# Building a graph layer's cell counts inside an earlier edge pass instead of next to their use

## The reference

```python
# attention layer
e = leaky_relu(a1[src] + a2[dst]); m = segment_max(e, dst)
ex = exp(e - m[dst]); out = segment_sum(ft[src] * ex / segment_sum(ex, dst)[dst], dst)
# mean layer
agg = segment_sum(x[edge_src], edge_dst)      # out = x @ W_self + (agg / deg) @ W_neigh + b
```

## Time and profile before

| | |
|---|---|
| median of 3 runs | 2354.08 us (2348.93 to 2357.85) |
| span of the profiled execution | 2350.5 us |
| busy | PE 1674.7, DVE 1397.8, POOL 1035.9, ACT 472.2 us |
| `stage_flash`, first gather to the next stage | 74 to 1124 us |
| `stage_experts` | 1124 to 1424 us |
| `blend` | 1424 to 1503 us |
| `stage_dense` | 1503 to 1900 us |
| `stage_experts2` and the output | 1900 to 2350 us |

### The profile page before, as it was taken

How to read it: one execution, slowest core, us unless ns; L and a number is a source line. 1 busy time by engine, 2 the same in 40 slices (tenths; PEclk the granted TensorE clock), 3 DMA queues, 4 the chain that set the end, 5 groups by cost and what they waited for, 6 DMA issues and landing times. The chain is left out here.

```text
span 2350.5 us, 34313 instructions
## 1 busy us (share of the span) xinstructions
PE 1674.7 (71%) x8967; PEld 1121.0 (48%) x8967; DVE 1397.8 (59%) x4277; ACT 472.2 (20%) x1077; POOL 1035.9 (44%) x1088
## 2 busy tenths in 40 slices
PE   4466666666667666666337993799999965599970
PEld 3222222222222222222226882599999964488860
DVE  6466666666666666667555115698888845211118
ACT  2100000000000000000322432533333312122222
POOL 1577777777777777773272332000000016222221
PEclk9677776776776767767558996899999976799985
DMA  7455555555555555553325863499000022566644
GB/s 203 108 145 145 142 145 138 144 142 142 145 144 144 145 145 145 145 144 92 99 97 153 246 211 130 103 246 244 2 0 0 0 48 83 160 214 215 214 140 160
DMA packets 255967, 321.42 MB, mean 137 GB/s; under 512 B 64440, under 2 KB 207522, under 8 KB 255767
## 3 DMA queue, kind: packets, MB, share of 16 engines
q1 hardware_dynamic: 198464, 174.84, 27.0%
q0 software_dynamic: 50208, 138.59, 21.6%
q10 hardware_dynamic: 7238, 7.39, 1.1%
HBM read 217.43 MB, written 103.68 MB: 137 GB/s over the span
## 5 line engine op out<-in xcount | busy, mean ns | idle before, releaser
L520 POOL DMA_INDIRECT f_buf<-ftab,scol x806 | 766.2, 951 | 288.5 <-issue 245.3
L920 PE MATMUL ps<-nb_parts,g_counts 128*120 128x256 bf16 x2550 | 305.9, 273 | 0.0
L603 PE MATMUL ps<-ident,f_left 128*128 128x512 f32 x204 | 189.5, 1084 | 135.5 <-ACT f_left L664 135.5
L920 PEld LDWEIGHTS ps<-nb_parts,g_counts 128*120 128x120 bf16 x2550 | 282.8, 133 | 1.9
L612 PE MATMUL ps<-f_diag,f_ones 128*128 128x512 f32 x204 | 186.7, 1070 | 88.6 <-DVE f_diag L754 88.6
L790 DVE TENSOR_TENSOR f_buf<-f_buf,ps 128x1024 f32<-128x1024 f32 x204 | 235.4, 1217 | 17.7 <-ACT ps L673 17.7
L1015 DVE TENSOR_SCALAR g_cell_hot<-nb_table,g_now 128x250 bf16<-128x250 int16 x816 | 231.9, 284 | 0.1
L1014 DVE TENSOR_SCALAR g_src_hot<-nb_table,g_now 128x128 bf16<-128x128 int16 x816 | 203.6, 249 | 27.8 <-PE ps L911 27.5
L751 DVE TENSOR_REDUCE ps<-ps 128x8 f32<-128x1024 f32 x51 | 62.9, 1233 | 250.0 <-PE ps L606 250.0
L1194 POOL MEMSET y_r_half<- 128x25 f32 x1 | 0.1, 120 | 415.1 <-POOLq L874 415.1
L952 ACT CAST g_counts<-ps 128x500 bf16<-128x500 f32 x204 | 115.0, 580 | 222.4 <-PE ps L911 221.3
(11 more groups left out here) (466 smaller groups left out, 2549.4 us busy)
## 6 DMA issues: line engine op xcount, KB each, us to landing
y_wts<-in_L_ffn_w_dram SPq DMA_DIRECT2D x68, 512.0 KB, 4.0
xs<-zero_rows SPq DMA_DIRECT2D x33, 1032.0 KB, 15.0
x_wts<-in_L_ffn_expert_w_dram SPq DMA_DIRECT2D x84, 256.0 KB, 3.2
xs<-zero_rows SPq DMA_DIRECT2D x51, 403.1 KB, 5.0
f_buf<-ftab,scol POOLq DMA_INDIRECT x806
y_xr<-xs SPq DMA_DIRECT2D x34, 258.0 KB, 3.8
x_xr<-xs SPq DMA_DIRECT2D x28, 258.0 KB, 3.1
f_st<-state SPq DMA_DIRECT2D x51, 132.5 KB, 2.3
```

Of the source, the lines that this page charges most:

```text
L520: nc.gpsimd.indirect_dma_start(out=buf[u][:, j, :], out_offset=None, in_=s.ftab, in_offset=bass.IndirectOffsetOnAxis(ap=s.scol[:, b * CB + ...
L603: nc.tensor.matmul(wide[:, w:w + 4, :], left[b.side][:].rearrange("p j h -> p (j h)"), bc(s.ident[:], 1, 4), start=True, stop=False)
L920: last = nc.tensor.matmul(acc[b.side], counts[b.side][:, t, :], s.parts[:, t, n, :], start=t == 0 and n == 0, stop=t == NT - 1 and n == PA ...
```

## The change

Counts are built in `stage_flash` and stored in DRAM; `stage_dense` loads and multiplies them.

- `stage_flash`, additions per batch. DVE: `cell_hots`, 16 one-hots of 250 columns from the int16 table in four pieces of four, and `bring_cells`. ACT: `bring_rows`, and `row_hots` in two halves, each 8 ACTIVATEs (Abs of iota minus the source row, 128 columns) and one ACTIVATE (Relu of 1 minus that, 1024 columns), which make `src_hot`; `lay` in four pieces. PE: `count` in four pieces of four matmuls. SP: `keep_counts`, one store of 128 x 4000 bytes.
- `stage_flash`, alterations. The diagonal (L754) and the one 16x1024 mask (L738) go. `spread_chunks` becomes 8 float32 transposes and 8 bfloat16 matmuls of 128 columns; `fold_chunks` becomes 2 bfloat16 matmuls of 512 columns and 8 float32 matmuls of 128 columns whose weights are the chunk maxima, broadcast. `mask_chunks` makes two 128x128 comparisons, and `bring` and `spread_tops` lose one instruction each. The two products share two PSUM banks, so the counts can have two.
- `stage_dense`. Ten blocks of 3 or 6 batches: 3, seven of 6, 3, 3. The features' parts are now the weights, 128 columns at a time, and the counts move, up to 480 columns: 150 matmuls a block. DVE adds each pair of chunks, 408 of them, to `accT` on its own (address read, add of 128 x 20, drain). ACT issues the loads of blocks ahead, and the first block is loaded during `blend`.
- `table_parts` is cut to `turn_parts`; its tables move into `stage_open`.

The orders in `stage_flash` after the change (the diff, cut to its core):

```diff
 # TensorE
                 def step(b, nxt, after, later):
                     bring(b)
+                    count(b, 0)
+                    look_up(b)
+                    count(b, 1)
                     if nxt:
                         spread_chunks(nxt)
-                    look_up(b)
-                    if nxt:
                         fold_chunks(nxt)
+                    count(b, 2)
+                    count(b, 3)
                     sum_up(b)
                     place_sums(b)
 # ScalarE
+            def row_hots(b, half):
+                n = CB // 2
+                act.wait_ge(built, b.quarter(2 * half + 1 - UNITS))
+                for j in range(n):
+                    nc.scalar.activation(rows_to[:, j, :], s.iota[:], ACT.Abs, bias=now_row[b.side][:, half * n + j:half * n + j + 1])
+                act.drain()
+                nc.scalar.activation(src_hot[:, half * n:(half + 1) * n, :], rows_to[:], ACT.Relu, scale=-1.0, bias=one[:]).then_inc(row_ready, UNITS // 2)
+                act.drain()
                 def step(b, nxt, after, later):
+                    lay(b, 0)
+                    lay(b, 1)
                     if nxt:
+                        bring_rows(nxt)
+                        row_hots(nxt, 0)
                         copy_left(nxt)
                     weigh(b)
+                    lay(b, 2)
+                    lay(b, 3)
                     if nxt:
+                        row_hots(nxt, 1)
                         fade(nxt)
                     keep_sums(b)
 # VectorE
+            def cell_hots(b, k):
+                dve.wait_ge(built, b.quarter(k - UNITS))
+                for j in range(k * UC, (k + 1) * UC):
+                    last = nc.vector.tensor_scalar(cell_hot[:, j, :], s.table[:], now_cell[b.side][:, j:j + 1], None, ALU.is_equal)
+                last.then_inc(hot_ready, 1)
                 def step(b, nxt, after, later):
+                    cell_hots(b, 0)
                     spread_tops(b)
                     if nxt:
                         mask_batch(nxt)
+                    cell_hots(b, 1)
+                    if nxt:
                         chunk_tops(nxt)
                     arguments(b)
+                    cell_hots(b, 2)
+                    cell_hots(b, 3)
                     messages(b)
                     if nxt:
+                        bring_cells(nxt)
                         batch_tops(nxt)
                     if after:
                         mask_chunks(after)
                     merge(b, nxt)
```

More of the change, by code:

```diff
@@ L87 @@
 NPS = 27 * 128
[L88 to L91, removed]
+GC = 2
+GB = CB // GC
+NGR = NC // GC
 UNITS = GB // 2
@@ L607, in spread_chunks @@
[L607 to L612, removed]
-                pe.wait_ge(masks_ready, b.count())
-                for h in range(0, HEADS, 4):
-                    last = nc.tensor.matmul(wide2[:, h:h + 4, :], s.nident[:], bc(bmask[b.side][:].rearrange("p j w -> p (j w)"), 1, 4), start=False, stop=True)
+                pe.wait_ge(mx_ready, b.count(1))
@@ new lines, in fold_chunks @@
+            def fold_chunks(b):
+                pe.wait_ge(mx_ready, b.count())
+                pe.wait_ge(masks_ready, b.count())
+                for w in range(0, W8, 4):
+                    nc.tensor.matmul(wide2[:, w:w + 4, :].rearrange("p w (j h) -> p w j h", h=HEADS), s.nident[:], bc(bmask[b.side][:, w:w + 4, :], 3, HEADS), start=True, stop=False)
+                for w in range(W8):
+                    last = nc.tensor.matmul(wide2[:, w, :], mx[b.side][:, w:w + 1].broadcast_to([128, 128]), s.ident[:], start=False, stop=w % 4 == 3)
@@ new lines, in _ @@
+            for m in range(len(BLOCKS)):
+                multiply(m)
+            pe.wait_ge(added, len(BLOCKS))
+            with pe.Fori(1, rounds2(pe)) as q:
+                with pe.Fori(0, NBT) as i:
+                    pe.wait_ge(late_hots, late(q, i))
+                    for j in range(CB):
+                        last = nc.tensor.matmul(late_cells[j // UC][:, j % UC // GC, :], src_hot[:, j, :], cell_hot[:, j, :], start=j % GC == 0, stop=j % GC == GC - 1)
+                    last.then_inc(late_built, 1)
+                    pe.wait_ge(late_laid, late(q, i))
+                    for c in range(2):
+                        for t in range(NT):
+                            for n in range(PARTS):
+                                last = nc.tensor.matmul(late_sums[c], s.parts[:, t, n, c * 128:(c + 1) * 128], counts[:, t, :],
+                                                        start=t == 0 and n == 0, stop=t == NT - 1 and n == PARTS - 1)
+                    last.then_inc(late_summed, 1)
@@ L959, in _ @@
[L959 to L967 removed]
+            for m in range(1, len(BLOCKS)):
+                lo, hi = BLOCKS[m]
+                if m >= 3:
+                    act.wait_ge(summed, m - 1)
+                act.dma_start(loaded[m % 2][:, 0:hi - lo, :], s.counts[lo:hi].rearrange("b p c -> p b c")).then_inc(arrived[m % 2], 16)
@@ L1005, in bring @@
-            def bring(b):
-                nc.vector.tensor_copy(now[b.side][:, 0, :], column(s.rcol, b, DB))
-                nc.vector.tensor_copy(now[b.side][:, 1, :], column(cell, b, DB))
-                dve.drain()
-            def hot(b, k):
-                dve.wait_ge(built, b.unit(k, UNITS))
-                for j in range(UC):
-                    at = k * UC + j
-                    nc.vector.tensor_scalar(src_hot[:, at, :], s.table[:, 0:128], now[b.side][:, 0, at:at + 1], None, ALU.is_equal)
-                    last = nc.vector.tensor_scalar(cell_hot[:, at, :], s.table[:], now[b.side][:, 1, at:at + 1], None, ALU.is_equal)
-                last.then_inc(hot_ready, 1)
@@ new lines, in _ @@
+            for m in range(len(BLOCKS)):
+                lo, hi = BLOCKS[m]
+                dve.wait_ge(summed, m + 1)
+                add_groups(lo * GB, (hi - lo) * GB, ps[:, 2 * (m % 2):2 * (m % 2) + 2, :])
+                dve.sem_inc(added, 1)
+            with dve.Fori(1, rounds2(dve)) as q:
+                late_turn()
+                with dve.Fori(0, NBT) as i:
+                    for row in range(2):
+                        nc.vector.tensor_copy(now[:, row, :], s.hots[:, row, bass.ds(i * CB, CB)])
+                    dve.drain()
+                    for j in range(CB):
+                        nc.vector.tensor_scalar(src_hot[:, j, :], s.iota[:], now[:, 1, j:j + 1], 0.0, ALU.add, ALU.is_equal)
+                        last = nc.vector.tensor_scalar(cell_hot[:, j, :], s.table[:], now[:, 0, j:j + 1], None, ALU.is_equal)
+                    last.then_inc(late_hots, 1)
+                    dve.wait_ge(late_summed, late(q, i))
+                    add_groups(i * GB, GB, ps[:, 0:2, :])
```

427 lines of the change are left out of this document (166 added, 261 removed).

## The result

The changed kernel takes 4147 us, median of 4 runs (4143.7 to 4152.9), against 2354.5 of the kernel before: ratio 1.763, interval 1.759 to 1.767. The forecast was 2582, in a range of 2430 to 2670. The direction was right and the size was not: 1793 us more instead of 228.

A forecast was written before the change was run, and what follows sets the result against it. Before, POOL's gathers bound stage_flash and PE bound stage_dense; after, a chain of waiting engines would bound stage_flash. 2350.5 + 347 - 119 = 2578.5, with the median 3.6 us above the span: 2582 us, range 2430 to 2670.

The forecast's parts named there:

- Stage_dense after: stage_dense: 260 products, 12.5 last adds, 5 second block's load, 1 start; 278 us against 397, 119 less.
- The adds: stage_dense, DVE: 0.52 us each; 24 adds, 12.5 us, stand behind the last matmul, the others hidden beside PE.
- bound of 0.64: stage_dense: if an add cost over 0.64 us, DVE would be the bound instead of PE.
- rival D: stage_dense: adds cost 0.8 us each, 341 us there instead of 278, 2645 in all; chance 0.08.
- its items: stage_flash chain per batch: DVE one-hots, PE counts, ACT row one-hots, PE spread, DVE maxima and messages, final add; 26.4 us.
- item 3: stage_flash, ACT: lays counts, brings rows, makes row_hots(nxt, 0) ahead of copy_left(nxt); 5.5 us a batch with hand-overs.
- waits at the port: stage_flash: DVE's one-hots blocked by GpSimd's gathers at the shared SBUF port add 0.3 to 0.6 us a batch.
- 347: stage_flash: us added by a period of 26.9 us a batch, 1471 instead of 1124; bounds 187 and 437.
- Each sign named for this stage: stage_flash: gathers wait some 6 us a batch, Abs directly before copy_left, DVE idle near 9 us, period 27 us.
- The sign named for `stage_dense`: stage_dense: PE without gaps for 260 us, then 12 us of adds.
- Rival A: stage_flash: POOL stays the bound if item 3's chain doesn't stand, copy_left ready before the gather; about 2262 us; chance 0.10.
- 2578.5: Whole kernel, profiled execution: 2350.5 plus 347 for stage_flash less 119 for stage_dense.

The follow-up runs named there:

- adds_lean: As after_lean, but DVE loads the addresses of 8 groups with one instruction ahead of 8 adds, without the check of their bounds: 2501.9 us.
- best_full: Changed kernel with a branch around late loops, addresses loaded by eight unchecked, copy_left before row_hots, spread_chunks before counts, SP's loops kept: 2236.7 us, 0.951 of the kernel before.
- after_lean: Changed kernel without the late loops of stage_dense, with SP's stream written out and window starts loaded four by one instruction: 2657.1 us, ratio 1.130.
- lean kernels: Kernels with SP's stream written out and window starts loaded four at once; the kernel before, so changed, took 2350.1 us, ratio 0.9995.
- first two sets: The first eight follow-up kernels, each set run beside the kernel before, which took 2577 and 2579 us there and 2352 in the last two sets.
- no_late: Changed kernel with the late rounds of stage_dense (loops from 1 to rounds2 on PE, ACT and DVE) left out: 3083.7 us.

## Why the prediction was wrong, and where it was right

**The step that failed is one that isn't there.** "Stage_dense after" sums products, adds, a load and a start; the loops from 1 to `rounds2` stand in the same function of the diff, and the text doesn't cost them. That puts them at nothing, without a reason. The runs showed a whole pass in their place: 1487 of the 1565 us between forecast and result. No row in the prediction shows it, since the loops over rounds in the kernel before start at 0 and run once. But its trace has what was needed, in the lines of DVE's loop in `stage_dense` (L1032):

```profile
L1032 DVEq MOVE  x2: 36/40/43, 1503.5 to 1503.6; - x2
L1032 DVEq COMPARE_BRANCH  x1: 55/55/55, 1899.2 to 1899.2; - x1
```

The one comparison stands at the end of the stage, behind the body, and none at its start. The other thing to do was to list the loop among the edits with its condition and a rival with its price: a pass is all counts, products and adds done serially.

**The adds were mis-sized.** The working had 0.27 for the address from the earlier trace rows, 0.17 for the add and 0.08 for the drain, 0.52 in all; it is 1.00 on average (71.8 busy and 337.3 of issue, by 408). The add is right, 0.176. But the earlier trace rows show only how long DVE was idle. The load, its register work and the check for that add (0.301, 0.204 and 0.023 us in the sequencer's own lines of the trace of before) ran while DVE still had one-hots to execute, and lay hidden behind them. In the changed kernel an add follows an add, nothing stands in front to hide them, and they show in full: the load is 0.30 or more, register work and check are 0.27 from start to start, and the drain is 0.18 and not 0.08. The text's own bound of 0.64 was then passed, and rival D's mechanism came true, in a stronger form than its 0.8. `adds_lean`, in which the adds are cheap, gives the sum as it stood: 276 us against 278, with PE at 260.43 against 260. The Trainium skill, page "DMA: Bandwidth & Descriptors", section "Latency and other measured facts", gives a floor of about 600 ns for such a load; the traces show less, 0.30 for one address and 0.60 for eight, and the measurement decides.

**`stage_flash` was right in mechanism and nearly in size.** By its items, forecast and then measured in the batch above: 3.1 and 3.1; 1.0 and 1.25; 5.5 and 5.3; 3.2 and 3.0; 11.8 and 11.2; 1.8 and 1.8. That is 26.4 and 25.6. In item 3 the Abs stand 0.29 us apart, where the working had 0.31. The 0.3 to 0.6 for waits at the port hardly show: 129 of the 816 one-hots last over 0.33 us, and all that the 816 last beyond their median is 16 us in the stage, 0.3 a batch at most, and hidden in part. 50 x 1.3 us are nearly all of the 68 by which 347 was too much. Each sign named for this stage came true: POOL's wait of 6 us, ACT's Abs directly ahead of `copy_left`, DVE's idle of 9.5 us ahead of the maximum. The sign named for `stage_dense`, PE without gaps for 260 us, did not: PE waited 125 us for the adds. Rival A, POOL as the bound, fell for this order of work, and `best_full` shows that it holds once the chain of item 3 is moved, as its condition said.

**Together:** 2578.5 less 68 and plus 153 is 2664, where `after_lean` has 2657; the pass makes it 4151. So with the pass counted, the two other errors would mostly have cancelled, and that is no merit of the sum.

**What stays open:** why SP is slow in two sets, whether that is the cause of the longer periods there or only comes with it, and whether fewer SP instructions would help; the sets with lean kernels didn't meet it.

## What to carry to other kernels

In these kernels a loop whose bound is read at run time runs its body at least once: one that is meant to do nothing for usual inputs needs a branch around it. Look in a trace where the loop's comparison stands, and in a prediction price each such loop in a diff, even where it looks empty. Small instructions at addresses from memory cost what the sequencer does between them (an add of 0.18 us took 1.0 here): load several addresses at once ahead of a group, and count load, register work, bound check and drain from their own lines. Work that is moved into a stage with idle engines should stand behind the copy or transpose on which the other engines wait: one line moved on ACT was worth 208 us.

## What the runs showed of the hardware that was not expected

In the first two sets SP's queue took about 0.70 us from instruction to instruction in stretches of some 20 of them, register instructions included, while the instructions of the other engines kept their durations. The loads of the window starts, in the profile after and then in `no_late`, whose SP stream is the same (ns, minimum/median/maximum):

```profile
L557 SPq FUSED_REGOPS  x212: 46/152/165, 84.5 to 1386.6; - x106
L557 SPq SEQ_ASSERT  x152: 18/18/31, 84.7 to 1386.8; - x152
```

```profile
L557 SPq FUSED_REGOPS  x212: 2/696/1384, 84.5 to 1799.6; - x106
L557 SPq SEQ_ASSERT  x152: 2/688/1422, 84.7 to 1799.8; - x152
```

The kernel before has 34.5 SP instructions a batch, and its period was 24.05 us there, which is 0.70 for each; the kernel after has 36.5, and its period was 33.4, so the count alone doesn't give it. In `no_late` the chunk maximum starts when SP's stretch ends, although no wait of the program joins them. So SP's pace may be the cause or another effect of the same cause, and neither was found. In these sets the kernel before was 9.6% slower, and a change that gained 208 us elsewhere gained 13.

And a granted clock of 0.81 in the blocks of `stage_dense` rose to 0.98 with the same matmuls, once DVE no longer made PE wait (`adds_lean`).
